# Running the patch embedding two tiles ahead, with a third patch buffer, in a fused ViT block kernel on one core

## What is computed

```
h = concat(cls_tok, patches(x) @ W.T + b)                 # 32 x 37 x 256
n = layernorm(h)
h = h + attention(n)      # 4 heads of 64: causal softmax part, mixed by sigmoid(betas) with
                          # a read of a memory, elu(q)+1 against mem and z; then @ Wo.T + bo
x = layernorm(h)
h = h + shared_expert(x) + sum over the 2 chosen of 8 experts of gate * expert(x)   # silu, hidden 1024
```

## Time and profile before

| | us |
|---|---|
| median of three executions | 340.05 |
| span of the profiled execution, first to last instruction | 337.0 |
| median less span (launch and end around it) | 3.05 |
| TensorE busy | 317.9 |
| VectorE, ScalarE, GpSimd busy | 224.1, 187.6, 146.3 |

### The profile page before, as it was taken

The page is one execution under the profiler, slowest core; times in us unless marked ns, Lnnn a source line. Parts: engine busy times, 40 slices in busy tenths (PEclk is TensorE's granted clock), DMA queues, the critical chain, the costliest instruction groups (busy, mean ns, idle before and its releaser), DMA issues.

```text
span 337.0 us, 9653 instructions
## 1 busy us (share of the span) xinstructions
PE 317.9 (94%) x3378; PEld 268.4 (80%) x3378; DVE 224.1 (66%) x497; ACT 187.6 (56%) x407; POOL 146.3 (43%) x224
## 2 busy tenths in 40 slices
PE   7789999999998898899999999999999999999990
PEld 6577888888887788799998777777787877777870
DVE  0234887888978888789979768675555555555540
ACT  1147767788777896756587788762323333232320
POOL 0455535655655336301271163645535353544131
PEclk9999999999999999999999999999999999999996
DMA  7592333326233101781689778234232323242221
GB/s 238 167 300 99 105 106 109 94 81 202 76 89 87 33 28 34 204 247 18 133 202 305 239 225 227 36 63 63 36 62 34 63 33 64 35 62 35 33 32 16
DMA packets 18612, 36.36 MB, mean 108 GB/s; under 512 B 3301, under 2 KB 10952, under 8 KB 18568
## 3 DMA queue, kind: packets, MB, share of 16 engines
q1 hardware_dynamic: 12136, 27.71, 25.8%
q0 software_dynamic: 6432, 8.03, 15.6%
HBM read 28.52 MB, written 7.21 MB: 106 GB/s over the span
## 4 chain that ended last, share of the span: by engine, by line
PE 83%; DVE 4%; DMA 3%; issue 3%; POOL 2%; ACT 2%; POOLq 1%; SPq 0%; DVEq 0%; ACTq 0%
PE bank L766 20%; PE bank L779 14%; PE bank L472 9%; PE bank L497 6%; PE bank L605 6%; PE bank L781 6%; PE bank L564 6%; PE bank L507 2%; DMA out_rows<-y,add_id 2%; PE bank L517 2%; PE bank L429 2%; PE bank L553 2%; PE bank L530 2%; PE bank L521 1%; DMA weights<-in_w_embed 1%
## 5 line engine op out<-in xcount | busy, mean ns | idle before, releaser
L766 PEld LDWEIGHTS bank<-x_t,weights 128*128 x1248 | 87.5, 98 | 25.6
L766 PE MATMUL bank<-x_t,weights 128*128 128x128 f16 x1248 | 103.9, 219 | 0.0
L944 ACT ACTIVATE act_out<-bank 128x512 f32<-128x512 f32 (+2 forms) x72 | 42.1, 586 | 87.7 <-PE bank L766 75.4
L779 PE MATMUL bank<-weights,hid_hi 128*128 x192 | 73.3, 382 | 0.3
L1172 POOL DMA_INDIRECT out_rows<-y,add_id x26 | 42.2, 1622 | 71.3 <-DVE y L1477 53.6
L1289 DVE SCALAR_TENSOR_TENSOR hid_lo<-act_out,hid_hi 128x512 f16<-128x512 f32 (+2 forms) x72 | 48.6, 680 | 13.1 <-ACT hid_hi L955 11.5
L781 PE MATMUL bank<-weights,hid_lo 128*128 x192 | 52.3, 273 | 0.0
L1295 DVE SCALAR_TENSOR_TENSOR weights<-stage,weights 128x1024 f16<-128x1024 f32 x36 | 42.9, 1219 | 0.4 <-ACT weights L908 0.2
L908 ACT ACTIVATE weights<-stage 128x1024 f16<-128x1024 f32 x36 | 36.8, 1049 | 0.0
L472 PE MATMUL bank<-weights 128*111 128x256 f32 x132 | 33.8, 411 | 1.0 <-DMA weights<-in_w_embed 1.0
L1139 POOL DMA_INDIRECT slot_rows<-x_rows,gather_id x26 | 27.5, 1058 | 12.7 <-DMA out_rows<-y 4.9
(11 more groups left out here) (142 smaller groups left out, 550.5 us busy)
## 6 DMA issues: line engine op xcount, KB each, us to landing
stage<-in_w_ffn SPq DMA_DIRECT2D x36, 512.0 KB
weights<-in_patches SPq DMA_DIRECT2D x11, 333.0 KB, 3.3
x_rows<-rows SPq DMA_DIRECT2D x11, 111.0 KB
out_rows<-weights SPq DMA_DIRECT2D x10, 111.0 KB
out_rows<-y POOLq DMA_DIRECT2D x9, 119.0 KB, 6.1
weights<-in_w_embed SPq DMA_DIRECT2D x3, 256.0 KB, 4.3
weights<-in_w_qk SPq DMA_DIRECT2D x1, 512.0 KB, 5.8
slot_rows<-x_rows,gather_id POOLq DMA_INDIRECT x26, 3.7
```

Source lines behind the costliest of these rows:

```text
L766: mm = nc.tensor.matmul(o, weights[:, bass.ds(base + 2 * k * CHUNK + 2 * (col - col % D) + w * D + col % D, P)], x_t[:, b, (2 * x + k) * P ...
L779: nc.tensor.matmul(bank[5 + b][0:m, :], hid_hi[:, b, c * P:c * P + m], weights[:, bass.ds(at, 2 * D)], start=(c == 0), stop=False)
L944: nc.scalar.activation(d_, s_, ACT.Silu, scale=1.0 / (X_SCALE * W_SCALE)).then_inc(hid_acted, 1)
```

## The change

Tile t's embedding is issued one step earlier: `embed(0)`, `embed(1)` and `embed(2)` in step 0, then `embed(s+2)` in the place of `embed(s+1)`; step 9 has no embedding. There are three patch buffers and seven buffers of h instead of two and six. The embedding of tile 2 has bank 3 and those from tile 3 on have the lower half of bank 4, whose upper half is `project_out`'s. `turn_xln` no longer waits for the next embedding's eviction; `project_out(t)` waits for it instead, and `embed(t)` waits for the eviction of the embedding before it and, from tile 7 on, for `residual(t-7)`. In steps 1 and 2 `turn_xln(s)` stands ahead of the embedding, in the others at the step's end as before. `embed_h` and `inv_std` run one tile further ahead too, and `embed_h(t)` waits for `inv_std(t-2)`, whose statistics it overwrites. On SP, `load_patches(2)` stands ahead of the projection matrices and waits for nothing; every later load waits for the embedding three tiles before.

```diff
-RING = 6
+RING = 7
+PATCH_RING = 3
         def embed_bank(t):
-            return bank[1][0:T, D:2 * D] if t else bank[4][0:T, 0:D]
+            if t == 1:
+                return bank[1][0:T, D:2 * D]
+            return bank[3 if t == 2 else 4][0:T, 0:D]
...
             def load_patches(t):
-                if t >= 2:
-                    sp.wait_ge(embed_ready, t - 1)
+                if t >= PATCH_RING:
+                    sp.wait_ge(embed_ready, t - PATCH_RING + 1)
...
             load_patches(1)
             sp.dma_start(s_id, ident).then_inc(ident_in, 16)
+            load_patches(2)
             sp.dma_start(s_wqk.rearrange("p a b c -> p (a b c)"), w_qk).then_inc(project_in, 16)
             sp.dma_start(s_wv.rearrange("p a b -> p (a b)"), w_v).then_inc(project_in, 16)
             sp.dma_start(s_ob[0:T], out_bias).then_inc(out_bias_in, 16)
-            load_patches(2)
...
 def turn_xln(t):
                 if t == 0:
                     pe.wait_ge(ident_in, 16)
-                pe.wait_ge(h_ready, min(t + 2, NT))
+                    pe.wait_ge(h_ready, 2)
...
             def embed(t):
-                pe.wait_ge(patches_in[t % 2], 16 * (t // 2 + 1))
-                if t >= 2:
-                    pe.wait_ge(xln_t_ready, t - 1)
+                pe.wait_ge(patches_in[t % PATCH_RING], 16 * (t // PATCH_RING + 1))
+                if t >= 3:
+                    pe.wait_ge(h_ready, t)
+                if t >= 7:
+                    pe.wait_ge(h2_ready, t - 6)
...
             def project_out(t):
                 pe.wait_ge(attn_t_ready, t + 1)
+                pe.wait_ge(h_ready, min(t + 7, NT))
...
                 if s == 0:
                     embed(0)
+                    embed(1)
...
-                embed(s + 1)
+                if 1 <= s < 3:
+                    turn_xln(s)
+                if s + 2 < NT:
+                    embed(s + 2)
...
-                turn_xln(s)
+                if s == 0 or s >= 3:
+                    turn_xln(s)
...
                 if s == 0:
                     inv_std(0, stats1, rstd1, 0, 1.0)
+                    inv_std(1, stats1, rstd1, 1, 1.0)
                     pool.wait_ge(out_bias_in, 16)
...
-                if s + 1 < NT:
-                    inv_std(s + 1, stats1, rstd1, (s + 1) % 2, 1.0)
+                if s + 2 < NT:
+                    inv_std(s + 2, stats1, rstd1, s % 2, 1.0)
...
             def embed_h(t):
                 dve.wait_ge(embed_ready, t + 1)
+                if t >= 2:
+                    dve.wait_ge(rstd1, t - 1)
...
                 if s == 0:
                     embed_h(0)
+                    embed_h(1)
...
-                if s + 1 < NT:
-                    embed_h(s + 1)
+                if s + 2 < NT:
+                    embed_h(s + 2)
```

More of the change, by code:

```diff
@@ L124, in build @@
         PATCH_CHUNK = EARLY * CHUNKS + used[0] // CHUNK
-        s_patch = part(2, PC, T)
+        s_patch = part(PATCH_RING, PC, T)
         h = part(RING, D)
@@ L192, in build @@
         route_in = sem("route_in")
-        patches_in = [sem(f"patches_in{i}") for i in range(2)]
+        patches_in = [sem(f"patches_in{i}") for i in range(PATCH_RING)]
         stage_in = [sem(f"stage_in{i}") for i in range(STAGES)]
@@ L358, in load_patches @@
             def load_patches(t):
-                if t >= 2:
-                    sp.wait_ge(embed_ready, t - 1)
-                sp.dma_start(s_patch[:, t % 2].rearrange("p a b -> p (a b)"),
-                             patches[t]).then_inc(patches_in[t % 2], 16)
+                if t >= PATCH_RING:
+                    sp.wait_ge(embed_ready, t - PATCH_RING + 1)
+                sp.dma_start(s_patch[:, t % PATCH_RING].rearrange("p a b -> p (a b)"),
+                             patches[t]).then_inc(patches_in[t % PATCH_RING], 16)
             load_patches(0)
@@ L471, in embed @@
                         pe.wait_ge(embed_in[k // (PC // EMBED_PARTS)], 16)
-                    mm = nc.tensor.matmul(embed_bank(t), s_patch[:, t % 2, k], s_we[:, k],
+                    mm = nc.tensor.matmul(embed_bank(t), s_patch[:, t % PATCH_RING, k], s_we[:, k],
                                           start=(k == 0), stop=(k == PC - 1))
```

## The result

The changed kernel is slower: 342.06 us against 339.47 us, medians of eight executions each, ratio 1.007 with a 95% interval of 1.0047 to 1.0094. The forecast was 339.3, no change. Against the sum's -0.73 us stand +2.6 us.

A forecast was written before the change was run, and what follows sets the result against it. TensorE was taken to bound the kernel, busy 317.9 of 337.0 us. Gains of 0.55 and 0.18 us (-0.73) made the span 336.3, and with 3.05 us around it 339.3 us, counted as no change; range 338.0 to 341.2.

The forecast's parts named there:

- the sum's -0.73 us: Whole kernel: 0.55 us of lead from the start plus 0.18 us gained in step 9.
- Part 4, the queues: SP and GpSimd queues: loads and reordered operations come in time; cost zero, bounds -0.1 and +0.5 us.
- Part 3, step 9: Step 9 without its embedding: TensorE idles about 2.4 of the 2.77 us taken out; gain 0.18 us, bounds 0 and 0.40.
- rival E: Step 9's idle time brings TensorE to 1.2 GHz, losing 4.45 us: 343.8 us, chance 0.08.
- Parts 1 and 2, the lead: Steps 0 to 2: filled idle times start project_qk(2) at 29.35 instead of 29.90, 0.55 us earlier; bounds 0.93 and 0.0.
- Steps 3 to 8: Same work per step with TensorE full, so the lead stays and the moved waits cost zero.
- F: Start: embedding 2 waits for its patches, 1.5 us late, and everything behind is late: 340.8 us, chance 0.07.
- B: Hand-written part behind the pipeline: ScalarE and VectorE pace it and the lead is lost there: 340.05 us, chance 0.15.
- C: VectorE's 1.0 us out of step 9 shortens its queue in steps it paces: 338.3 us, chance 0.2.
- D: Step 9: no idle time, so the whole 2.77 us is won on top of 0.55: 336.7 us, chance 0.05.
- The rule that spoke against the change: TensorE falls to half clock after idleness until sustained work; step 9's 2.4 us idle might cost more than itself.

The follow-up runs named there:

- e1: The changed kernel run again with nothing edited, to see the granted clock of each execution: 342.2 us, ratio 1.0075 to the kernel before.
- e2: The changed kernel with step 9's idle time filled by wasted work, tile 10's six embedding products run a second time: 341.11 us, ratio 1.0038 to the kernel before.
- e3: The changed kernel with tile 10's embedding put back into step 9, so the idle time moves to step 8: 342.46 us, ratio 1.0065 to the kernel before.
- e7: The changed kernel, loads unaltered, with step 9 filled by due work in the order of the hand-written part: 339.6 us, ratio 1.0009 to the kernel before.
- e5: The changed kernel with loads of patches 3 and 4 issued ahead of the routing constants, step 9 unaltered: 339.11 us, ratio 0.9973 to the kernel before.
- e6: As e5, with step 9 also filled by tile 10's embedding products run a second time: 336.83 us, ratio 0.9931 to the kernel before.
- e9: The kernel before run again with nothing edited, for its granted clock: 339.56 us, ratio 0.9999.
- e4: The kernel before with five of the six products of tile 10's embedding left out, giving step 9 an idle time: 339.11 us, ratio 1.002.
- e11: As e5, with step 9 filled by only three of the six wasted products: 336.84 us, ratio 0.9925 to the kernel before.

## Why the prediction was wrong, point by point

**Part 4, the queues, costed at zero with an upper bound of +0.5: wrong, and the first cause.** The step that failed is "the constants, patches 3 and the four first weight chunks go out some 4 us earlier". Patches 3 and the chunks went out 0.75 us earlier in the first profile and 0.1 to 0.3 us earlier in e1, e2, e3 and e7 (16.89 to 17.14 against 17.23), since SP was held at its issues (2.45 and 2.37 us in the first). The landing time of up to 7.8 us was nearly right (8.3 measured for patches 4), but added to a wrong time of issue, 15.5 where it was 18.87. The check of each load against its need was made for patches 2 and 4, and left out for patches 3, whose consumer moves by 6 us. The waits measured 0.70 to 3.36 us for patches 3; undoing them is worth 2.7 to 3.1 us in the median (e1 to e5), the fall of the clock behind them among it.

**Part 3, step 9: right in the trace, mis-sized in the time.** 2.36 us of idle time, ended by the exponentials. From the start of the scores to the mixed values it is 3.00 us (90.25 to 93.25), before 3.26 (89.94 to 93.20): 0.26 gained, less 0.06 for the restart, so 0.20 where 0.18 was forecast. What it costs through the clock was only rival E, with 0.08. It is the likeliest case: eight of twelve executions in e5, where no other idle time as long is left. Its price was too high: 4.45 us were taken from the slow spell at the start, while a fall in the steps loses 1.7 us of TensorE's time in e1, and the two groups of e5 lie some 3 us apart. (Falls of longer duration were seen too: in e5's profile 20 us from 90 on have a mean clock of 0.83, which is 3.4 us.) Median to median, e5 to e6, it is 2.3 us. The sentence "It decides if 2.4 us idle are enough where 1.47 us are not" was built on one profile. By the mean clocks, the idle time of step 0 (1.47 and 1.71 us in two profiles) is enough in 50 of 71 executions. The profile of the kernel before was also of a short execution: every execution here lies 1.8 to 1.9 us above its span (338.8 and 336.9 after the change), so the profiled one before took about 338.8 us, not 340.05, and the 3.05 us around it were 1.8 to 1.9.

**Parts 1 and 2, the lead: right in kind, too low.** Without late loads (e5), from the end of embedding 1 (14.93 - 2.77 = 12.16) to project_qk(2) at 28.26 it is 16.10 us, against 29.90 - 12.88 = 17.02 before: 0.92 us, where 0.55 was taken and 0.93 was the bound (the 2.77 stands for one embedding, as in the forecast). The short wait for the eviction ahead of project_qk(2) came, 0.30 us. In the after profile project_qk(0) is at 15.87 (forecast 16.30), since the first three embeddings were through at 4.55 + 10.70 = 15.25, and project_qk(1) is at 22.35 (22.0), where the first wait for patches already counts. The two embeddings of e5 that start with no idle time ahead of them take 2.6 us rather than 2.77 (18.49 to 21.08 and 24.82 to 27.41).

**Steps 3 to 8 at zero: right.** From project_qk(2) at 30.29 to the scores of step 9 at 90.25 it is 59.96 us, before 29.90 to 89.94, 60.04. The moved waits cost nothing.

**The rivals.** F (a load is late, 0.07) and E (0.08) both came, together, and together they were given too little. E came in the place named. F came in another: it was named for embedding 2, which starts without a wait in the profile after, and it came at embedding 3 and once at embedding 4, by the queueing of Part 4. B, C and D did not. In e6's profile project_qk(10) starts 1.10 us earlier than in that of the kernel before (103.76 and 104.86), and the span is 1.3 us shorter (335.7 and 337.0): the lead reaches the end, and nothing like C's further 1.0 us is added. The range, 338.0 to 341.2, ends short of 342.06 because E was left out of it and the two rivals together stood in no case.

**The rule that spoke against the change.** In the runs here the granted clock falls to 0.50 behind idle times of 1.71 us (e9), 2.02 and 2.36 us (e1) and 2.36 us (e3, e5), and stays at 1.00 behind 1.47 us (before), 1.74 us (e4), 2.36 us (after), 2.69 us (e7) and 3.36 us (e2). The length alone doesn't decide it in one execution. The Trainium skill (TensorE: Matmul & The Clock Gate, Part 1: The HAM clock gate) says that the chip's watch over the array's activity runs freely and isn't tied to the kernel's start. By that, the same idle time is caught in one execution and not in the next; the groups of executions of the same program in e4 and e5 agree, but no run here shows the watch itself.

**What adds up, and what doesn't.** The two causes do not simply add. Against the kernel before in the same batch, the medians are +2.55 us with late loads and the hole (e1), +1.46 with late loads alone (e2), -0.17 with the hole alone (e5) and -2.45 with neither (e6). So filling the hole is worth 1.1 us with late loads and 2.3 us without, and mending the loads 2.7 us with the hole and 3.9 us without. With the loads mended alone, e5 comes out at 339.11, near the forecast 339.3, but not by the forecast's sum: a larger lead and the missing fall of the kernel before are set off against the fall that the hole brings.

Where the gain of e11 and e6 over the kernel before comes from is shown by the profiles of e9 (339.7 us, near the median of the kernel before) and of e11 (336.74 us, near its own), from the same batch. Of e11:

```profile
4.70 10.28 PE L479 MATMUL bank<-weights 128*111 128x256 f32 x36 [1.05 <-DMA weights<-in_w_embed]
...
28.31 2.04 PE L504 MATMUL bank<-weights 128*128 128x111 f32 x16 [0.30 <-ACT weights L872]
```

Of the 2.96 us between them, 2.62 are there at project_qk(2) already (30.93 and 28.31). From the end of embedding 1 to that place e9 needs 30.93 - 12.02 = 18.91 us, the profile of the kernel before, without a fall, 17.02, and e11 28.31 - (14.98 - 2.77) = 16.10. So 0.92 us are the lead. The 1.89 us are the kernel's own affair: 0.24 for its longer wait for the norm (1.71 and 1.47) and, from project_qk(0) to project_qk(2), 16.36 against 14.70, 1.66 for the fall. Of these 2.81 us, 0.19 are lost again because e11's first embeddings ended later. The remaining 0.3 us lie behind project_qk(2). The two groups of the kernel before lie only 1.2 us apart, less than this: in e9 embedding 1 ended 0.86 us sooner than in the first profile (12.02 and 12.88), which pays back part of the fall. Whether the two go together in other executions was not seen.

## What to carry to other kernels

Work taken out of a step to do it earlier leaves a hole there; ask what it covered, and put due work in its place before the move is judged. When consumers move forward, check every load against its new need with the issue time that the queue can reach, not the one that its waits allow. And a single profile shows one of several executions. The mean clock of each execution beside its time (0.996 in the profiled one, 0.982 to 0.991 in the other seven) says that there is something which the profile does not show.

## What the runs showed of the hardware that was not expected

- TensorE's clock falls with a delay: 1.2 to 1.8 us after the idle time has ended and the engine is busy again (in e1 idle until 94.87, and a clock of 0.83 from 96 to 97 puts the fall at about 96.7), for about three and a half microseconds there. In e5 it fell sooner, in the microsecond in which work resumed, and lasted longer.
- The row of the granted clock says nothing of the slow start. In the profile of the kernel before it stands at 1.00 from 8 to 9 us, where TensorE does four matmuls of the embedding in the microsecond, as at 0.50 in e1 (22 to 23); from 10 us on it does six. So the mean clock does not count the start either, and executions of one mean clock can still differ there.
- Wasted matmuls in an idle time made a kernel 2.3 us faster (e5 to e6), and half of them did as much (e11).
- SP's issue of a small transfer (32 KB) took 2.45 to 3.01 us when about 2.9 MB had been issued in the 5.4 us before it (in the profiles of after, e1, e2, e3, e5 and e7), and 0.33 us in the kernel before. What holds it was not tried.
